# Convolution stage: three two-bank kernel buffers in PSUM instead of two, one pair sum moved from VectorE to GpSimd, and new places for the other stages' work

## The chip, the cores and the metric

One Trainium2 chip, one core of it. The time is device microseconds of one execution; the kernel before took 5519.98 us (median of three runs, 5519.80 to 5520.31). The input is eight images of 128 channels and 128 x 128 points in float32.

## The reference, cut to what matters

The first layer mixes tokens in 8 x 8 windows (attention and an MLP). The change does not touch it. The second layer, which the change is about, is

```python
enh  = conv3x3_depthwise(conv1x1(x))                       # 128 channels, 9 taps each
h    = conv3x3_grouped(x)          # 16 channels
h1, h2 = split(h, 2)
attn = conv1x1(h1 * h2) * attgamma + conv1x1(x)            # 16 coefficients per point
# kba: at every point the 16 coefficients give, by selfw, a 2 x 18 kernel for each
# pair of channels, applied to the 3 x 3 neighbourhood of enh; and, by selfb, a bias
x2   = kba(enh, attn) * ga1 + enh
out  = x2 + x
```

## The kernel before

**Tiling.** After the first layer (to about 1855 us) `convolve` (L773) works through 64 bands of 16 image rows, 8 to an image. A band is four chunks of 4 rows x 128 points, that is 512 columns, one PSUM bank. Channels lie on the 128 partitions.

**The main loop.** A chunk needs nine taps, so a band has 36 kernel products, numbered q = 0 to 35. For each, TensorE multiplies two 128 x 128 basis matrices by the band's 512 coefficients (`basis_kernels`, L1035) and leaves two banks of kernels: one for the channel itself, one for its partner in the pair. VectorE multiplies the two banks by the shifted rows of `enh` (`product`, L1259). A product goes either to a place in SBUF, tile `products`, or back over its own kernels in PSUM. In the second case VectorE adds it to the next product (`merge`, L1265; list `VECTOR_MERGES`, ten of them). Six more pairs are summed by GpSimd from SBUF (`merge`, L959; list `POOL_MERGES`). What is left, 20 terms of two halves each for a band, TensorE transposes and accumulates in a bank `ps_t` (`add_half`, L1055, four 128 x 128 transposes a half), together with one half for the input rows `x_own`. Then ScalarE copies the sum to SBUF (`sum_out`, L1149), TensorE adds the bias and transposes it back into the same bank (`back`, L1065 and L1067), and ScalarE copies the chunk out (`chunk_out`, L1154).

**The other stages.** Four bands are in work at once: l, m = l - 1, n = m - 1 and o = n - 1. TensorE computes the pointwise convolution (`pointwise`, L994), which ScalarE copies to `e0` (`e0_rows`, L1119); the grouped convolution (`group_taps`, L1017, 36 matmuls with 32 output rows each; the trace has two instructions for each float32 matmul, so 72 a band); and the coefficients (`coefficients`, L1024). ScalarE scales the nine depthwise taps of each half band (`tap_product`, L1174 and L1169), and GpSimd adds them up into `enh` (`add_tap`, L953), 16 additions a band; four tap buffers lie between the two. VectorE makes `h_prod` (L1279) and `att_lo` (L1283) once a band. SyncE's queue moves half of `h_sb` to other partitions, spreads the coefficients (16 small transfers), keeps two edge rows in DRAM, and loads and stores.

**Order.** Each engine's order is written out by hand. One pass over the 46 operations of VectorE's list `OPS` is a band; position in it is the slot. TensorE first issues in a slot the kernels whose buffer operation `slot` frees (`KERNEL_SLOT`), and waits for that operation. After that come the halves of `HALF_SLOT` and `X_SLOTS`, then `BACK_SLOTS`, `CONV_SLOTS`, the coefficients, and `PW_SLOTS`. A slot number of 46 or more means the next pass. ScalarE's taps stand at `TAP_PLACES` among the same slots; GpSimd's sums stand at `POOL_MERGE_PLACES` among its 16 additions.

**PSUM.** Eight banks: two kernel buffers of two banks (`ps_k`), two banks for sums (`ps_t`, chunk j uses number j % 2), one for the pointwise convolution (`ps_p`), one for the grouped convolution and the coefficients (`ps_m`). With two kernel buffers, the kernels of a product are issued after the operation that stands one before the last user of the other buffer.

Of the kernel before, what the change touches and what calls it, by code (L numbers as in the profile page):

```python
# [19 lines left out]
ALU = mybir.AluOpType  # L20
# [61 lines left out]

HALF_SLOT = {0: 10, 1: 7, 6: 6, 7: 6, 8: 11, 9: 9, 14: 11, 15: 11, 16: 12, 17: 12, 20: 15, 21: 19, 24: 15, 25: 18, 26: 25, 27: 25, 32: 22, 33: 22, 34: 22, 35: 22, 38: 26, 39: 28, 40: 31, 41: 31, 46: 33, 47: 32, 48: 37, 49: 37, 52: 35, 53: 35, 56: 38, 57: 38, 58: 44, 59: 44, 64: 44, 65: 43, 68: 47, 69: 48, 70: 47, 71: 47}


X_SLOTS = [16, 25, 38, 48]

# [685 lines left out]
def convolve(nc, prepared, x2, out):  # L773
# [4 lines left out]
    with ExitStack() as ctx:  # L778
# [33 lines left out]
        first_banks = [ps_p, ps_t[0], ps_t[1], ps_p, ps_t[0]]  # L812

# [43 lines left out]
        with nc.Block() as block:  # L857
            @block.sync
            def _(sp):
# [45 lines left out]
                def step(items, p):  # L905
                    l, m, n, o = items
                    b = 1 - p
                    if n is not None:
                        load_own(n, 0)
                    if o is not None:  # L910
                        store(o, CHUNKS - 1)
                    if l is not None and not (isinstance(l, int) and l == 0):
                        loads(l, p)
                    if n is not None:
                        load_own(n, 1)
                    if n is not None and not (isinstance(n, int) and n == bands - 1):
                        keep_edge(n, p)
                    if m is not None and not (isinstance(m, int) and m == 0):
                        fetch_edge(m, b)
                    if m is not None:  # L920
                        move_h2(m)
                    if n is not None:
                        store(n, 0)
                    if m is not None:
                        attention_rows(m, b)
                    if isinstance(m, int) and m == 0:
                        keep_top_rows()
                        fetch_edge(m, b)
                    if n is not None:
                        store(n, 1)  # L930
                        store(n, 2)
# [45 lines left out]
            def _(pe):  # L977
# [7 lines left out]
                def pointwise(m, p, c):  # L985
                    if c == 0:
                        pe.wait_ge(x_in[p], rounds(m, p, 16) + 16)
                    first = isinstance(m, int) and m == 0
                    if not first:
                        pe.wait_ge(e0_ready, PW_CHUNKS * m + c)  # L990
                    elif c > first_banks.index(first_banks[c]):
                        pe.wait_ge(e0_ready, first_banks.index(first_banks[c]) + 1)
                    lo, hi = PAD + CHUNK_ROWS * c, min(PAD + CHUNK_ROWS * (c + 1), XROWS)
                    nc.tensor.matmul((first_banks[c] if first else ps_p)[:, 0:W * (hi - lo)], pwT[:, :], xin[p][:, lo:hi, 1:W + 1],  # L994
                                     start=True, stop=True).then_inc(pw_done, 1)
# [10 lines left out]
                def group_taps(m, p, first, last):  # L1006

                    for i in range(first, last):
                        t, j = divmod(i, CHUNKS)
                        if i == 0:  # L1010
                            pe.wait_ge(x_in[p], rounds(m, p, 16) + 16)
                            pe.wait_ge(edges_ready, 1)
                            pe.wait_ge(grouped_ready, 1)
                            at_least(pe, att_lo_ready, m)
                        dy, dx = divmod(t, 3)
                        r = 1 + CHUNK_ROWS * j + dy
                        mm = nc.tensor.matmul(ps_m[32 * j:32 * j + 32, :], gT[:, t, :], xin[p][:, r:r + CHUNK_ROWS, dx:dx + W],  # L1017
                                              start=(t == 0), stop=(t == TAPS - 1))
                        if i == TAPS * CHUNKS - 1:
                            mm.then_inc(conv_done, 1)  # L1020
# [5 lines left out]
                def basis_kernels(n, p, q):  # L1026
                    if q == 0 and isinstance(n, int) and n == 0:
                        pe.wait_ge(basis_ready, 2)
                        pe.wait_ge(top_step, (TAPS - 3) * len(top_groups))
                    if q == 0:  # L1030
                        pe.wait_ge(att_in[p], rounds(n, p, 256) + 256)
                    j, t = divmod(q, TAPS)
                    at_least(pe, product_ready, SLOTS_IN_BAND * n + KERNEL_FREE[q])
                    for s in range(2):
                        mm = nc.tensor.matmul(ps_k[KERNEL_BUFFER[q] ^ (SWAPPED & p)][:, BANK * s:BANK * (s + 1)], basis[:, 2 * t + s, :],  # L1035
                                              att[p][:, j, :], start=True, stop=True)
                    mm.then_inc(k_done, 1)

                def add_half(n, j, half):
# [11 lines left out]
                    if start:  # L1051
                        at_least(pe, out_ready, CHUNKS * n + j - 1)
                    for r in range(CHUNK_ROWS):
                        rows = x_own[j // 2][:, CHUNK_ROWS * (j % 2) + r, :] if q == Q else products[:, PLACE[q], s, C * r:C * (r + 1)]
                        mm = nc.tensor.matmul(ps_t[j % 2][:, C * r:C * (r + 1)], rows, (ident, ident_swap)[s][:, :], is_transpose=True,  # L1055
                                              start=(start and r == 0), stop=(stop and r == CHUNK_ROWS - 1), skip_group_check=True)
# [51 lines left out]
            def _(act):  # L1108
# [3 lines left out]
                def e0_rows(m, p, c):  # L1112
# [4 lines left out]
                    lo, hi = PAD + CHUNK_ROWS * c, min(PAD + CHUNK_ROWS * (c + 1), XROWS)  # L1117
                    ps = (first_banks[c] if isinstance(m, int) and m == 0 else ps_p)[:, 0:W * (hi - lo)]
                    nc.scalar.activation(e0[p][:, lo:hi, 1:W + 1], ps.rearrange("c (h w) -> c h w", w=W), ACT.Identity,  # L1119
# [26 lines left out]
                def sum_out(n, j):  # L1146
                    act.wait_ge(sum_done, CHUNKS * n + j + 1)
                    at_least(act, back_done, CHUNKS * n + j - 1)
                    nc.scalar.activation(summedT[j % 2][:, :], ps_t[j % 2][:, :], ACT.Copy).then_inc(sumT_ready, 1)  # L1149

                def chunk_out(n, j):
                    act.wait_ge(back_done, CHUNKS * n + j + 1)
                    at_least(act, stored[j], 16 * n)
                    nc.scalar.activation(out_sb[:, CHUNK_ROWS * j:CHUNK_ROWS * (j + 1), :],  # L1154
                                         ps_t[j % 2][:, :].rearrange("c (h w) -> c h w", w=W), ACT.Copy).then_inc(out_ready, 1)

# [46 lines left out]
            def _(dve):  # L1203
# [38 lines left out]
                def product(n, p, q):  # L1242
# [9 lines left out]
                    dve.wait_ge(k_done, Q * n + q + 1)  # L1252
                    kernels = ps_k[KERNEL_BUFFER[q] ^ (SWAPPED & p)][:, :].rearrange("c (s h w) -> c s h w", s=2, w=W)
                    if q in VECTOR_MERGES:
# [7 lines left out]
                def merge(n, p, q):  # L1262
                    dve.wait_ge(product_ready, SLOTS_IN_BAND * n + OP_COUNT["product", q + 1])
                    both = products[:, PLACE[q + 1], :, :].rearrange("c s w -> c (s w)")
                    nc.vector.tensor_tensor(both, ps_k[KERNEL_BUFFER[q] ^ (SWAPPED & p)][:, :], both, ALU.add).then_inc(product_ready, 1)  # L1265

# [56 lines left out]
```

## Time and profile before

The profiled execution took 5518.02 us; its span, from the first to the last instruction, is 5515.9 us. The granted clock of TensorE was 0.996 of full speed over the span.

| engine | busy over the span | busy, 3000 to 4000 us |
|---|---|---|
| TensorE, matmuls | 5377.8 us (97%) | 982 of 1000 us |
| TensorE, weight loads | 3907.0 us (71%) | 663 |
| VectorE | 5149.3 us (93%) | 976 |
| ScalarE | 3324.5 us (60%) | 515 |
| GpSimd | 4237.7 us (77%) | 876 |

Matmuls overlap in the array and their ends are modelled, so a matmul's duration is longer than the time until the next one can start; where a sum is wanted, take the distance of starts. VectorE's operations overlap by some 0.1 us too. "Idle before" names what the engine waited for. The convolution stage is 64 alike bands, so a time for one band, multiplied by 64, is the stage.

### The profile page before, as it was taken

What the parts mean: (1) busy time and instruction counts of PE and PEld (TensorE: products, weight loads), DVE (VectorE), ACT (ScalarE), POOL (GpSimd) and SP (SyncE); (2) the same over time, 40 slices, a digit from 0 to 9 for tenths busy, and PEclk for the clock granted to TensorE, in tenths of its full rate; (3) what the DMA queues carried; (4) which work ended last, traced back from release to release, by engine and by line L of the source; (5) the groups of instructions that cost most, each with busy time, mean ns of one, the idle gap of its engine ahead of it and who ended that gap; (6) DMA issues with size and microseconds to landing.
All of it is one profiled execution on the core that took longest, in us unless ns stands there. A gap on an engine that the chain in (4) does not pass through costs nothing.

```text
span 5515.9 us, 112725 instructions
## 1 busy us (share of the span) xinstructions
PE 5377.8 (97%) x37904; PEld 3907.0 (71%) x37904; DVE 5149.3 (93%) x5424; ACT 3324.5 (60%) x4094; POOL 4237.7 (77%) x1958
## 2 busy tenths in 40 slices
PE   8999999999999799999999999999999999999998
PEld 7888888888888466666666666666666666666666
DVE  7888888888888699999999999999999999999999
ACT  6888888888888554555555554555555554555553
POOL 4655565556555688888888888888888888888886
PEclk9999999999999899999999999999999999999999
DMA  3222222222222222222222222222222222222221
GB/s 92 74 76 76 71 74 76 76 71 73 76 76 68 78 71 83 69 79 74 73 81 73 79 71 81 69 79 73 72 81 73 79 72 81 70 80 72 72 81 47
DMA packets 175616, 413.21 MB, mean 75 GB/s; under 512 B 37201, under 2 KB 58769, under 8 KB 175505
## 3 DMA queue, kind: packets, MB, share of 16 engines
q1 hardware_dynamic: 175568, 412.59, 24.5%
q8 instruction: 29, 0.48, 0.0%
q14 instruction: 19, 0.15, 0.0%
HBM read 228.94 MB, written 145.77 MB: 68 GB/s over the span
## 4 chain that ended last, share of the span: by engine, by line
PE 48%; DVE 12%; issue 5%; POOL 1%; DVEq 0%; ACT 0%; POOLq 0%
PE ps_k L1035 18%; PE ps_t L1055 15%; PE ps_m L1017 9%; DVE products L1259 6%; PE ps_p L994 3%; DVE products L1265 3%; DVE ps_k L1259 2%; PE ps_t L1067 2%; PE ps_t L1065 1%; POOL enh L953 1%; DVE h_prod L1279 1%; DVEq L133 0%; DVEq L1252 0%; DVEq L1277 0%; PE ps_t L994 0%
## 5 line engine op out<-in xcount | busy, mean ns | idle before, releaser
L953 POOL TENSOR_TENSOR enh<-enh,tap 128x1024 f32<-128x1024 f32 x1024 | 2263.0, 2210 | 68.0 <-ACT tap L1174 9.3
L1259 DVE TENSOR_TENSOR products<-ps_k,enh 128x1024 f32<-128x1024 f32 x1664 | 1997.7, 1218 | 53.3 <-PE ps_k L1035 39.6
L1035 PE MATMUL ps_k<-att,basis 128*128 128x512 f32 x4608 | 1682.8, 449 | 80.6 <-DVE products L1265 56.5
L1174 ACT ACTIVATE tap<-e,dw 128x1024 f32<-128x1024 f32 x1024 | 1147.5, 1146 | 313.2 <-POOL enh L953 312.0
L486 POOL TENSOR_TENSOR hidden_lo<-hidden,hidden_hi 128x1024 fp32r<-128x1024 f32 x256 | 693.3, 2729 | 717.5 <-DVE hidden_hi L691 717.5
L959 POOL TENSOR_TENSOR products<-products 128x1024 f32<-128x1024 f32 x384 | 915.9, 2392 | 418.2 <-DVE products L1259 418.2
L1035 PEld LDWEIGHTS ps_k<-att,basis 128*128 128x128 f32 x4608 | 707.1, 189 | 689.7 <-DVE products L1259 409.7
L1265 DVE TENSOR_TENSOR products<-ps_k,products 128x1024 f32<-128x1024 f32 x640 | 783.7, 1225 | 21.8
L1259 DVE TENSOR_TENSOR ps_k<-ps_k,enh 128x1024 f32<-128x1024 f32 x640 | 784.5, 1226 | 20.5 <-PE ps_k L1035 3.8
L1055 PE MATMUL ps_t<-ident_swap,products 128*128 128x128 f32 x5120 | 736.6, 272 | 0.7 <-POOL products L959 0.7
L1055 PE MATMUL ps_t<-ident,products 128*128 128x128 f32 x5120 | 724.9, 272 | 0.1
L1055 PEld LDWEIGHTS ps_t<-ident,products 128*128 128x128 f32 x5120 | 616.6, 141 | 113.0 <-DVE products L1265 0.3
L1055 PEld LDWEIGHTS ps_t<-ident_swap,products 128*128 128x128 f32 x5120 | 603.0, 141 | 68.9 <-issue 32.8
L1017 PE MATMUL ps_m<-xin,gT 128*32 128x512 f32 x4608 | 592.0, 606 | 0.0
L1149 ACT ACTIVATE summedT<-ps_t 128x512 f32<-128x512 f32 x256 | 153.2, 598 | 677.9 <-PE ps_t L1055 677.6
L1154 ACT ACTIVATE out_sb<-ps_t 128x512 f32<-128x512 f32 x256 | 152.4, 595 | 522.0 <-PE ps_t L1067 522.0
L656 ACT ACTIVATE hidden<-ring,bias 128x512 f32<-128x512 f32 x512 | 350.7, 690 | 176.0 <-PE ring L514 175.0
L708 DVE CAST x_hi<-xt 128x512 fp32r<-128x512 f32 x256 | 407.4, 1632 | 48.2 <-PE ring L514 48.1
L511 PE MATMUL ring<-x_hi,w_hi 128*128 128x512 f32 x1024 | 419.0, 409 | 6.3 <-ACT hidden L656 3.7
L491 POOL TENSOR_TENSOR x_lo<-xt,x_hi 128x512 fp32r<-128x512 f32 x256 | 377.9, 1497 | 55.6 <-DVE x_hi L708 55.6
L514 PE MATMUL ring<-x_lo,w_hi 128*128 128x512 f32 x1024 | 404.4, 395 | 0.4 <-POOL x_lo L491 0.4
L512 PE MATMUL ring<-x_hi,w_lo 128*128 128x512 f32 x1024 | 403.6, 394 | 0.0
(115 smaller groups left out, 7273.9 us busy)
## 6 DMA issues: line engine op xcount, KB each, us to landing
xin<-layer_out SPq DMA_DIRECT2D x64, 1280.0 KB, 7.3
xt<-in_x SPq DMA_DIRECT2D x128, 512.0 KB, 4.1
layer_out<-xo SPq DMA_DIRECT2D x128, 512.0 KB, 2.9
x_own<-layer_out SPq DMA_DIRECT2D x128, 512.0 KB, 4.0
out<-out_sb SPq DMA_DIRECT2D x256, 256.0 KB, 2.0
att<-att_hi SPq DMA_DIRECT2D x512, 32.0 KB, 2.0
att<-att_lo SPq DMA_DIRECT2D x512, 32.0 KB, 2.0
enh<-edge_rows SPq DMA_DIRECT2D x64, 130.0 KB, 2.1
```

The costliest lines, as they stand in the source:

```text
L486: nc.gpsimd.tensor_tensor(hidden_lo[:, h, :, :], hidden[:, h, :, :], hidden_hi[:, h, :, :].bitcast(FP32), ALU.subtract).then_inc(hidden_lo ...
L511: nc.tensor.matmul(out, w_hi[:, w, :], hi, start=start, stop=False)
L514: return nc.tensor.matmul(out, w_hi[:, w, :], lo, start=False, stop=stop)
L708: nc.vector.tensor_copy(windows(x_hi[:, PAIRS * h:PAIRS * (h + 1), :]), half_windows(xt[p], h)).then_inc(x_hi_ready, 1)
L953: nc.gpsimd.tensor_tensor(own, own, tap_sb[add % TAP_BUFFERS][:, 0:hi - lo, :], ALU.add).then_inc(dw_done, 1)
L959: nc.gpsimd.tensor_tensor(lead, lead, products[:, PLACE[q + 1], :, :], ALU.add).then_inc(pool_merged, 1)
L1017: mm = nc.tensor.matmul(ps_m[32 * j:32 * j + 32, :], gT[:, t, :], xin[p][:, r:r + CHUNK_ROWS, dx:dx + W], start=(t == 0), stop=(t == TAPS ...
L1035: mm = nc.tensor.matmul(ps_k[KERNEL_BUFFER[q] ^ (SWAPPED & p)][:, BANK * s:BANK * (s + 1)], basis[:, 2 * t + s, :], att[p][:, j, :], start ...
L1055: mm = nc.tensor.matmul(ps_t[j % 2][:, C * r:C * (r + 1)], rows, (ident, ident_swap)[s][:, :], is_transpose=True, start=(start and r == 0) ...
L1174: nc.scalar.activation(tap_sb[add % TAP_BUFFERS][:, 0:hi - lo, :], src, ACT.Copy, scale=dw[:, t:t + 1]).then_inc(tap_ready, 1)
L1259: nc.vector.tensor_tensor(out, kernels, enh[p][:, r:r + CHUNK_ROWS, dx:dx + W].unsqueeze(1).to_broadcast([C, 2, CHUNK_ROWS, W]), ALU.mult) ...
L1265: nc.vector.tensor_tensor(both, ps_k[KERNEL_BUFFER[q] ^ (SWAPPED & p)][:, :], both, ALU.add).then_inc(product_ready, 1)
```

## The change

The diff, with blank lines and renamed uses of the same expression left out:

```diff
-VECTOR_MERGES = (2, 6, 9, 11, 15, 18, 22, 27, 31, 33)
-POOL_MERGES = (0, 4, 13, 20, 24, 29)
+VECTOR_MERGES = (2, 6, 11, 16, 18, 22, 27, 31, 33)
+POOL_MERGES = (0, 4, 9, 13, 20, 24, 29)
+KERNEL_BUFFERS = 3
-KERNEL_BUFFER = {0: 0, 1: 1}
-for q in range(2, Q):
-    KERNEL_BUFFER[q] = KERNEL_BUFFER[FREEING[q - 2][1]]
-SWAPPED = KERNEL_BUFFER[FREEING[-2][1]]
-KERNEL_FREE = {q: FREEING[q - 2][0] if q >= 2 else FREEING[q - 2][0] - SLOTS_IN_BAND for q in range(Q)}
+KERNEL_BUFFER = {q: q for q in range(KERNEL_BUFFERS)}
+for q in range(KERNEL_BUFFERS, Q):
+    KERNEL_BUFFER[q] = KERNEL_BUFFER[FREEING[q - KERNEL_BUFFERS][1]]
+NEXT_ORDER = [KERNEL_BUFFER[q] for _, q in FREEING[-KERNEL_BUFFERS:]]
+KERNEL_FREE = {q: FREEING[q - KERNEL_BUFFERS][0] - (SLOTS_IN_BAND if q < KERNEL_BUFFERS else 0) for q in range(Q)}
...
-X_SLOTS = [16, 25, 38, 48]
+X_SLOTS = [13, 23, 38, 48]
-BACK_SLOTS = [21, 34, 40, 51]
+BACK_SLOTS = [14, 25, 41, 50]
-POOL_MERGE_PLACES = (0, 0.6000000000000001, 3.0, 6.0, 9.5, 10.9)
+POOL_MERGE_PLACES = (0, 1.5, 3, 5.5, 9.5, 11.5, 13.4)
-TAP_PLACES = ((0.5, 1.5, 3.0, 5.5, 10.5, 13.0, 13.5, 14.0, 19.5), (22.0, 24.5, 27.0, 28.0, 31.0, 35.5, 36.5, 36.5, 41.5))
-CLEAR_PLACE = 64
-H_PROD_SLOT = 27
-ATT_HIGH = 28
-ATT_LOW = 33
-CONV_SLOTS = [33, 33, 42, 42, 42, 42, 46, 46, 50, 50, 54, 54, 59, 59, 59, 59, 66, 66]
-COEFFICIENT_SLOT = 28
-PW_SLOTS = [17, 19, 27, 30, 36]
+TAP_PLACES = ((0.0, 0.0, 2.0, 3.0, 3.5, 6.0, 6.5, 7.0, 11.5), (15.0, 16.5, 19.0, 20.5, 24.5, 30.5, 31.0, 31.5, 37.4))
+CLEAR_PLACE = 58
+H_PROD_SLOT = 8
+ATT_HIGH = 6
+ATT_LOW = 12
+CONV_SLOTS = [24, 24, 26, 26, 26, 26, 33, 33, 33, 33, 36, 36, 41, 41, 41, 41, 45, 45]
+COEFFICIENT_SLOT = 8
+PW_SLOTS = [12, 13, 15, 17, 22]
...
-        ps_k = [bank(f"ps_k{i}", 2) for i in range(2)]
-        ps_t = [bank(f"ps_t{i}") for i in range(2)]
-        ps_p = bank("ps_p")
+        ps_k = [bank(f"ps_k{i}", 2) for i in range(KERNEL_BUFFERS)]
+        ps_t = bank("ps_t")
         ps_m = bank("ps_m")
...
 def step(items, p):                      # SyncE's queue, one pass
     load_own(n, 0)
-    store(o, CHUNKS - 1)
-    loads(l, p)
-    load_own(n, 1)
-    keep_edge(n, p)
-    fetch_edge(m, b)
-    move_h2(m)
-    store(n, 0)
-    attention_rows(m, b)
-    store(n, 1)
-    store(n, 2)
+    move_h2(m)
+    loads(l, p)
+    store(o, CHUNKS - 1)
+    load_own(n, 1)
+    attention_rows(m, b)
+    keep_edge(n, p)
+    fetch_edge(m, b)
+    store(n, 0)
+    store(n, 1)
+    store(n, 2)
...
 def pointwise(m, p, c):                  # now into ps_m
                     if not first:
                         pe.wait_ge(e0_ready, PW_CHUNKS * m + c)
+                        if c == 0:
+                            pe.wait_ge(att_lo_ready, m)
...
 def group_taps(m, p, first, last):       # i == 0
-                            at_least(pe, att_lo_ready, m)
+                                pe.wait_ge(e0_ready, PW_CHUNKS * m + PW_CHUNKS)
...
 def add_half(n, j, half):                # all chunks in the one bank ps_t
                     if start:
-                        at_least(pe, out_ready, CHUNKS * n + j - 1)
+                        at_least(pe, out_ready, CHUNKS * n + j)
```

`HALF_SLOT` is also new throughout. By it and the lists above, the sums of chunks 0 to 3 are transposed in slots 6 to 13, 16 to 23, 29 to 38 and 43 to 48, and go back in slots 14, 25, 41 and 50. Before, the sum of the next chunk could begin ahead of the way back of the one in hand (chunk 1 from slot 15, chunk 0 back in slot 21). VectorE's list now has 45 operations, 36 products and 9 sums; the transposed terms are still 20.

## Rows read from the trace of the kernel before

**Rows 1.** Page, busy time by engine (us, share, instructions).
```profile
PE 5377.8 (97%) x37904; PEld 3907.0 (71%) x37904; DVE 5149.3 (93%) x5424; ACT 3324.5 (60%) x4094; POOL 4237.7 (77%) x1958
```
**Rows 2.** Waits, 2000 to 5000 us (us in total, times, longest us).
```profile
POOL products L959 <- DVE products L1259: 330.1, 160, 4.2
PEld ps_k L1035 <- DVE products L1259: 327.2, 637, 0.9
...
DVE products L1259 <- PE ps_k L1035: 33.1, 106, 0.5
```
**Rows 3.** VectorE in order (start us, us), and `h_prod` 43 bands later.
```profile
3007.51 0.74 DVE L1279 SCALAR_TENSOR_TENSOR h_prod<-ps_m,bias_h,h_up 128x512 f32<-128x512 f32 x1
3008.17 1.22 DVE L1259 TENSOR_TENSOR ps_k<-ps_k,enh 128x1024 f32<-128x1024 f32 x1
3009.30 1.22 DVE L1259 TENSOR_TENSOR products<-ps_k,enh 128x1024 f32<-128x1024 f32 x1
3010.55 1.22 DVE L1265 TENSOR_TENSOR products<-ps_k,products 128x1024 f32<-128x1024 f32 x1
3011.69 3.55 DVE L1259 TENSOR_TENSOR products<-ps_k,enh 128x1024 f32<-128x1024 f32 x3
...
5432.11 0.74 DVE L1279 SCALAR_TENSOR_TENSOR h_prod<-ps_m,bias_h,h_up 128x512 f32<-128x512 f32 x1
```
**Rows 4.** VectorE, the first and the last product of the stage.
```profile
1900.56 2.36 DVE L1259 TENSOR_TENSOR products<-ps_k,enh 128x1024 f32<-128x1024 f32 x2 [8.63 <-DMA enh<-edge_rows]
...
5507.63 1.22 DVE L1259 TENSOR_TENSOR products<-ps_k,enh 128x1024 f32<-128x1024 f32 x1
```
**Rows 5.** TensorE in order of time, a stretch with each kind of work.
```profile
3024.57 0.40 PE L1065 MATMUL ps_t<-att,basis 128*128 128x512 f32 x1
...
3030.22 0.60 PE L1055 MATMUL ps_t<-ident,products 128*128 128x128 f32 x4
3030.58 1.21 PE L1035 MATMUL ps_k<-att,basis 128*128 128x512 f32 x4
3031.72 1.07 PE L1017 MATMUL ps_m<-xin,gT 128*32 128x512 f32 x8
3032.73 0.73 PE L1035 MATMUL ps_k<-att,basis 128*128 128x512 f32 x2
3033.30 1.03 PE L1055 MATMUL ps_t<-ident,products 128*128 128x128 f32 x8
3034.17 1.04 PE L1055 MATMUL ps_t<-ident_swap,products 128*128 128x128 f32 x8
```
**Rows 6.** TensorE in order of time, one chunk of the pointwise convolution.
```profile
3012.40 1.02 PE L994 MATMUL ps_p<-xin,pwT 128*128 128x512 f32 x2
3012.96 0.93 PE L1035 MATMUL ps_k<-att,basis 128*128 128x512 f32 x2
```
**Rows 7.** GpSimd in order of time, part of a band.
```profile
3024.09 13.64 POOL L953 TENSOR_TENSOR enh<-enh,tap 128x1024 f32<-128x1024 f32 x6
3037.70 4.74 POOL L959 TENSOR_TENSOR products<-products 128x1024 f32<-128x1024 f32 x2
3042.40 6.75 POOL L953 TENSOR_TENSOR enh<-enh,tap 128x1024 f32<-128x1024 f32 x3
```
**Rows 8.** ScalarE in order: a tap, and the two copies around one way back.
```profile
3021.30 1.15 ACT L1174 ACTIVATE tap<-e,dw 128x1024 f32<-128x1024 f32 x1
...
3023.15 0.60 ACT L1149 ACTIVATE summedT<-ps_t 128x512 f32<-128x512 f32 x1 [0.33 <-PE ps_t L1055]
3025.44 0.60 ACT L1154 ACTIVATE out_sb<-ps_t 128x512 f32<-128x512 f32 x1 [1.69 <-PE ps_t L1067]
```
**Rows 9.** SyncE's queue: the moves of `h_sb` in the same band.
```profile
3001.69 2.74 SPq L888 DMA_DIRECT2D h_up<-h_sb  x4
```
**Rows 10.** DMA issues by size (KB each, median us to landing).
```profile
xin<-layer_out SPq DMA_DIRECT2D x64, 1280.0 KB, 7.3
...
att<-att_hi SPq DMA_DIRECT2D x512, 32.0 KB, 2.0
```

More of the change, by code:

```diff
@@ L62 @@
 SLOTS_IN_BAND = len(OPS)
+KERNEL_BUFFERS = 3
 FREEING = [(OP_COUNT[op], op[1]) for op in OPS if op[0] == "merge" or op[1] not in VECTOR_MERGES]
-KERNEL_BUFFER = {0: 0, 1: 1}
-for q in range(2, Q):
-    KERNEL_BUFFER[q] = KERNEL_BUFFER[FREEING[q - 2][1]]
-SWAPPED = KERNEL_BUFFER[FREEING[-2][1]]
-KERNEL_FREE = {q: FREEING[q - 2][0] if q >= 2 else FREEING[q - 2][0] - SLOTS_IN_BAND for q in range(Q)}
+KERNEL_BUFFER = {q: q for q in range(KERNEL_BUFFERS)}
+for q in range(KERNEL_BUFFERS, Q):
+    KERNEL_BUFFER[q] = KERNEL_BUFFER[FREEING[q - KERNEL_BUFFERS][1]]
+NEXT_ORDER = [KERNEL_BUFFER[q] for _, q in FREEING[-KERNEL_BUFFERS:]]
+assert [NEXT_ORDER[i] for i in NEXT_ORDER] == list(range(KERNEL_BUFFERS))
+KERNEL_FREE = {q: FREEING[q - KERNEL_BUFFERS][0] - (SLOTS_IN_BAND if q < KERNEL_BUFFERS else 0) for q in range(Q)}
 KERNEL_SLOT = {q: KERNEL_FREE[q] - 1 for q in range(Q)}
@@ L92 @@
 POOL_TERM_COUNT = {q: i + 1 for i, q in enumerate(sorted(POOL_MERGES, key=LAST_HALF.get))}
-BACK_SLOTS = [21, 34, 40, 51]
+BACK_SLOTS = [14, 25, 41, 50]
 POOL_PLACES = 2 * (TAPS - 1)
-POOL_MERGE_PLACES = (0, 0.6000000000000001, 3.0, 6.0, 9.5, 10.9)
-TAP_PLACES = ((0.5, 1.5, 3.0, 5.5, 10.5, 13.0, 13.5, 14.0, 19.5), (22.0, 24.5, 27.0, 28.0, 31.0, 35.5, 36.5, 36.5, 41.5))
-CLEAR_PLACE = 64
-H_PROD_SLOT = 27
-ATT_HIGH = 28
-ATT_LOW = 33
-CONV_SLOTS = [33, 33, 42, 42, 42, 42, 46, 46, 50, 50, 54, 54, 59, 59, 59, 59, 66, 66]
-COEFFICIENT_SLOT = 28
-PW_SLOTS = [17, 19, 27, 30, 36]
+POOL_MERGE_PLACES = (0, 1.5, 3, 5.5, 9.5, 11.5, 13.4)
[7 more added lines that the diff above has]
+PW_SLOTS = [12, 13, 15, 17, 22]
+assert all(HALVES_OF[j][0][0] > BACK_SLOTS[j - 1] for j in range(1, CHUNKS)) and HALVES_OF[0][0][0] + SLOTS_IN_BAND > BACK_SLOTS[-1]
+assert all(BACK_SLOTS[j] > HALVES_OF[j][-1][0] for j in range(CHUNKS))
+assert PW_SLOTS[-1] < CONV_SLOTS[0] and SLOTS_IN_BAND <= CONV_SLOTS[-1] <= COEFFICIENT_SLOT + SLOTS_IN_BAND and COEFFICIENT_SLOT <= PW_SLOTS[0]
+assert BACK_SLOTS[-1] - SLOTS_IN_BAND < COEFFICIENT_SLOT
 def at_least(engine, semaphore, value):
@@ L909, in step @@
                         load_own(n, 0)
+                    if m is not None:
+                        move_h2(m)
+                    if l is not None and not (isinstance(l, int) and l == 0):
+                        loads(l, p)
                     if o is not None:
                         store(o, CHUNKS - 1)
[L912 to L913 removed]
                     if n is not None:
                         load_own(n, 1)
[L916 to L923 removed]
                     if m is not None:
@@ L928, in step @@
                         fetch_edge(m, b)
+                    if n is not None and not (isinstance(n, int) and n == bands - 1):
+                        keep_edge(n, p)
+                    if m is not None and not (isinstance(m, int) and m == 0):
+                        fetch_edge(m, b)
                     if n is not None:
+                        store(n, 0)
                         store(n, 1)
@@ L990, in pointwise @@
                         pe.wait_ge(e0_ready, PW_CHUNKS * m + c)
-                    elif c > first_banks.index(first_banks[c]):
-                        pe.wait_ge(e0_ready, first_banks.index(first_banks[c]) + 1)
+                        if c == 0:
+                            pe.wait_ge(att_lo_ready, m)
+                    elif c >= 3:
+                        pe.wait_ge(e0_ready, c - 2)
                     lo, hi = PAD + CHUNK_ROWS * c, min(PAD + CHUNK_ROWS * (c + 1), XROWS)
-                    nc.tensor.matmul((first_banks[c] if first else ps_p)[:, 0:W * (hi - lo)], pwT[:, :], xin[p][:, lo:hi, 1:W + 1],
+                    nc.tensor.matmul((first_banks[c] if first else ps_m)[:, 0:W * (hi - lo)], pwT[:, :], xin[p][:, lo:hi, 1:W + 1],
                                      start=True, stop=True).then_inc(pw_done, 1)
@@ L1029, in basis_kernels @@
                         pe.wait_ge(top_step, (TAPS - 3) * len(top_groups))
+                        pe.wait_ge(e0_ready, PW_CHUNKS)
                     if q == 0:
@@ L1034, in basis_kernels @@
                     for s in range(2):
-                        mm = nc.tensor.matmul(ps_k[KERNEL_BUFFER[q] ^ (SWAPPED & p)][:, BANK * s:BANK * (s + 1)], basis[:, 2 * t + s, :],
+                        mm = nc.tensor.matmul(ps_k[NEXT_ORDER[KERNEL_BUFFER[q]] if p else KERNEL_BUFFER[q]][:, BANK * s:BANK * (s + 1)], basis[:, 2 * t + s, :],
                                               att[p][:, j, :], start=True, stop=True)
@@ L1117, in e0_rows @@
                     lo, hi = PAD + CHUNK_ROWS * c, min(PAD + CHUNK_ROWS * (c + 1), XROWS)
-                    ps = (first_banks[c] if isinstance(m, int) and m == 0 else ps_p)[:, 0:W * (hi - lo)]
+                    ps = (first_banks[c] if isinstance(m, int) and m == 0 else ps_m)[:, 0:W * (hi - lo)]
                     nc.scalar.activation(e0[p][:, lo:hi, 1:W + 1], ps.rearrange("c (h w) -> c h w", w=W), ACT.Identity,
@@ L1252, in product @@
                     dve.wait_ge(k_done, Q * n + q + 1)
-                    kernels = ps_k[KERNEL_BUFFER[q] ^ (SWAPPED & p)][:, :].rearrange("c (s h w) -> c s h w", s=2, w=W)
+                    kernels = ps_k[NEXT_ORDER[KERNEL_BUFFER[q]] if p else KERNEL_BUFFER[q]][:, :].rearrange("c (s h w) -> c s h w", s=2, w=W)
                     if q in VECTOR_MERGES:
@@ L1264, in merge @@
                     both = products[:, PLACE[q + 1], :, :].rearrange("c s w -> c (s w)")
-                    nc.vector.tensor_tensor(both, ps_k[KERNEL_BUFFER[q] ^ (SWAPPED & p)][:, :], both, ALU.add).then_inc(product_ready, 1)
+                    nc.vector.tensor_tensor(both, ps_k[NEXT_ORDER[KERNEL_BUFFER[q]] if p else KERNEL_BUFFER[q]][:, :], both, ALU.add).then_inc(product_ready, 1)
                 def step(items, p):
```

15 lines of the change are left out of this document (8 added, 7 removed).

## The prediction, written before the changed kernel was run

> **What bounds the kernel now.** I read the page's busy times first, then the waits of the steady stretch, then each engine in order of time. The page puts TensorE at 97% and VectorE at 93% of the span [rows 1], which settles nothing: matmul durations overlap. The waits say more. In 3000 us, 53 bands, TensorE's weight loads for the kernels stood 637 times for a VectorE product, while VectorE stood for TensorE only 106 times, 33 us, 0.6 us a band [rows 2]. So each band mostly goes at VectorE's pace, and TensorE is the one that comes early. VectorE's stage is also nearly all of what the change touches: its first product starts at 1900.56 and its last at 5507.63 [rows 4], and 43 bands take 5432.11 - 3007.51 = 2424.6 us [rows 3], so a band takes 56.39 us.
>
> What does VectorE need for a band, if nothing holds it? By distance of starts [rows 3]: product into PSUM 1.13 (3008.17 to 3009.30), product ahead of its sum 1.25, the sum 1.14, so a summed pair costs 3.52; a product with no sum 1.13; `h_prod` 0.66, and `att_lo`, which is the same kind, as much. Before: 10 x 3.52 + 16 x 1.13 + 1.3 = 54.6 us. The other 1.8 us of the 56.39 are lost: 0.6 in the waits named above, the rest in delays too short for the wait list, most of them, I take it, kernels that come a little late, because with two buffers TensorE may only be one operation behind.
>
> TensorE's need for a band [rows 5, 6]: 36 kernel pairs at 0.57 (two in 3030.58 to 3031.72) = 20.5; 44 half transpositions (40 of terms, 4 of input rows) at 0.435 (two in 3033.30 to 3034.17) = 19.1; the grouped convolution, nine runs of eight at 1.01 = 9.1; five pointwise chunks and the coefficients at 0.56 = 3.4; four ways back at one matmul (0.285) and four transpositions (0.435) = 2.9. Sum 55.0. A half just ahead of kernels takes only 0.36 (3030.22 to 3030.58), and 17 or so a band stand there: -1.3. That gives 53.7, and it may be 1 us too much, because the distances of kernels and of the grouped convolution can hold small waits. So TensorE is within 1 to 2.5 us of VectorE, and nothing that VectorE saves beyond that can reach the clock.
>
> GpSimd [rows 7]: an addition 2.27 (six in 13.61), a sum 2.35. Before: 16 x 2.27 + 6 x 2.35 = 50.4, and it waits for VectorE 330 us in 53 bands, 6.2 a band [rows 2]; together 56.6, which is the band.
>
> **The rule and the row.** The Trainium skill says in "Perfetto Trace Analysis", section "Identifying the Most-Contended Engine", that matmul occupancy is a poor measure and that TensorE's headroom should be judged by weight-load busy time. The row has 71% [rows 1], so by the rule TensorE would need some 40 us a band and could never bind; my sum from distances of starts says 53.7. By the rule the result would be VectorE's bound below with certainty; I don't follow it, and leave the sum as it is.
>
> **The change, part by part.**
>
> *One sum less on VectorE.* The pair of q = 9 goes to GpSimd; those of 15 to 17 only change partners. 9 x 3.52 + 18 x 1.13 + 1.3 = 53.3 us, which is 1.26 less a band. That is the floor of the stage.
>
> *The third kernel buffer.* Every product now has its kernels issued at least two operations ahead (2.27 us less 0.57 for the pair) instead of one. A heavy slot of TensorE (slots 3, 17, 29, 31, 35 hold 1.9 to 2.6 us of work against 1.13 of VectorE) no longer shows on VectorE by itself. At best all 1.8 us of losses go, at worst none. TensorE's extra lead gives nothing when its own sum is the longer one. VectorE at 53.3 and TensorE at 52.7 to 53.7, each with waits of its own, should end close above the larger: I take 54.0 a band, that is 0.7 of the 1.8 stay, since both engines will now be about equally full.
>
> *One sum more on GpSimd.* 16 x 2.27 + 7 x 2.35 = 52.8, in a band of 54.0. It fits with 1.2 to spare. Its first addition of a pass waits for two taps on ScalarE, which start when VectorE begins the band (1.23 + 1.15, some 2.5 us [rows 8] for the second), and the last ends near 55: it overlaps the next pass by 1, so that it hardly rests. Its sums come late by it: q = 13 is ready at about 25.2 us and TensorE wants it in slot 19 at 24.5; q = 20 at 36.5 against 36.1. Such waits of 0.4 to 0.7 lie where TensorE has a light slot. Cost taken: 0; up to 1 us if TensorE has no slack. Durations of VectorE's operations I leave alone: sums read one operand from PSUM as before.
>
> *One sum bank.* A handover is: copy 0.60, way back 0.87 (3024.57 to the copy's start at 3025.44), copy 0.60 = 2.1 us at least, 2.9 as it stood at 3023.15 to 3026.04 [rows 5, 8]; with a tap of 1.15 in front of each copy 4.4. The new lists leave from the last half of a chunk to the first of the next three slots (13 to 16, 48 to 51, that is 3.4 us), six (23 to 29) and five (38 to 43). Two are long enough with a tap in front of both copies, the other two only with 1.3 us of ScalarE's delay. Inside them TensorE has kernels and pointwise work, so a delay costs only what exceeds that. Taken: 0.2 a band, inside the 54.0; bounds 0 and 2.3 (one tap in front of a copy in each short handover).
>
> *The attention chain moves from slots 20 to 33 to slots 0 to 12.* The grouped convolution ends in slot 0, ScalarE copies, SyncE issues four moves. Before, `h_prod` started 5.8 us after the first move's issue [rows 3, 9] without a wait; the moves need 2.74 to issue [rows 9] and about 2.0 to land [rows 10]. After, the convolution ends about 3.3 us into the band, the copy at 4.2, the moves have landed at 9.0; VectorE reaches slot 8's end at 10.3. It is covered by 1.3 us. Were it late, VectorE itself, with all its products queued behind, would stand. Taken 0, up to 1.0. The coefficients then wait for `h_prod` (0.7 after slot 8), and behind them TensorE has halves and kernels that are wanted two operations later: 0.
>
> *Pointwise in ps_m.* Its first chunk waits for `att_lo`, 0.66 after slot 12; TensorE spends 0.57 of it on kernels. Chunks 0 and 1 stand one slot apart, with a ScalarE copy between them; three halves (1.3 us) cover it. 0.2, bound 1.2 (one tap ahead of that copy).
>
> *SyncE's queue.* `move_h2` is now second, so it can't stand behind an edge or a store. The band's load of 1280 KB, behind it, is issued at 7.0 and needs 7.3 [rows 10]: 14.3, against 16.2 for slot 12 with `att_lo`. 0, bound 0.5. Edge rows and stores have half a band to spare. In the first band the load is issued after the first `h_sb` copy; VectorE's start hangs on the edge rows [rows 4], so I change nothing there, with a bound of 5 us in all.
>
> **The sum.** 56.39 - 54.0 = 2.39 us a band, 64 bands: 153 us. 5518.02 - 153 = 5365 us; the median shown is 2 us above the profiled execution: 5367.
>
> **The rivals.**
> 1. *TensorE becomes the bound.* For: its 53.7, and that it keeps all its work. It adds the waits for `att_lo`, `e0` and the two short handovers, 1.0 to 2.5 together: 54.7 to 56.2, middle 55.4, that is 5457. Against: many of its waits fall where it was early anyway.
> 2. *GpSimd becomes the bound.* 52.8 and the 2.5 of the first tap, if that is not overlapped: 55.3, 5450. Against: it may run over into the next pass.
> 3. *The third buffer brings nothing*: the losses are not late kernels. 55.1, 5440.
> 4. *The one sum bank makes it slower.* From TensorE's 53.7 the kernel is slower once the four handovers leave it idle for over 0.7 each; at 1.0 each, 57.7 a band, it is 5604. For: ScalarE is in order, and a tap that waits for GpSimd stands in front of a copy for longer than its own 1.15. Against: the taps placed before each copy are due well behind the additions that free their buffers.
>
> **How the numbers follow.** Mine 0.62 (53.3 to 54.7 a band, 5322 to 5412); TensorE 0.18; GpSimd 0.06; no use of the buffer 0.05; the slower case 0.09. The range goes from the floor 53.3 (5322) to 55.4 (5457), where the first rival's middle lies. What a measurement of this kernel tells from no change is about 0.2%, 11 us: within it only the edge of rivals 1 and 4, 0.03; slower 0.07; faster 0.90.
>
> **What would show it.** In the trace after, `h_prod` to `h_prod` should be 54.0. VectorE waiting for TensorE should fall under 0.3 us a band, and GpSimd's wait from 6.2 to under 2. The weight loads of kernels should stand less for VectorE than before. I am wrong if VectorE stands for `ps_k` by over 1 us a band (rival 1), for `moved` at `h_prod`, if GpSimd's sums hold up the transpositions, or if TensorE idles before the first half of a chunk with ScalarE's `out_sb` as releaser (rival 4).

## The result, and the profile after

The changed kernel takes 5359.64 us (median of 4 runs, 5359.02 to 5362.06) against 5520.15 us before: ratio 0.971, 95% interval 0.9693 to 0.9727. The forecast was 5367 us, faster, range 5322 to 5457. The profiled execution is the slowest of the four, 5362.06 us; its span is 5360.3 us, 155.6 less than before.

The page, busy time by engine, against [rows 1]: VectorE has 64 instructions less, GpSimd 64 more, TensorE as many.

```profile
PE 5267.2 (98%) x37904; PEld 3936.0 (73%) x37904; DVE 5032.0 (94%) x5360; ACT 3322.0 (62%) x4094; POOL 4373.8 (82%) x2022
```

VectorE in order of time, `h_prod` in one band and 41 bands later, against [rows 3]:

```profile
3051.43 0.74 DVE L1301 SCALAR_TENSOR_TENSOR h_prod<-ps_m,bias_h,h_up 128x512 f32<-128x512 f32 x1
...
5257.04 0.74 DVE L1301 SCALAR_TENSOR_TENSOR h_prod<-ps_m,bias_h,h_up 128x512 f32<-128x512 f32 x1
```

2205.6 us over 41 is 53.80 us a band, 2.59 less than before; forecast was 54.0. The busy times of 2000 to 5000 us of the changed kernel (us from the start, width, then TensorE, its weight loads, VectorE, ScalarE, GpSimd, granted clock, DMA share, GB/s):

```profile
2000.00:5000.00 3000.00, 2985.52 (x19634) 2105.78 (x19627) 2967.68 (x2622) 1612.56 (x1895) 2867.33 (x1283) 1.00 0.26 79
```

TensorE is free for 14.5 us in 56 bands, 0.26 a band, and that is one wait: the first half of chunk 0 for ScalarE's copy of the chunk before. The waits of the same stretch, against [rows 2]:

```profile
POOL enh L971 <- ACT tap L1196: 97.6, 56, 1.9
PEld ps_k L1057 <- DVE products L1281: 88.9, 105, 0.9
...
PE ps_t L1077 <- ACT out_sb L1176: 14.5, 56, 0.3
DVE ps_k L1281 <- PE ps_k L1057: 12.5, 56, 0.3
```

The weight loads of kernels stood for VectorE 327 us for its products alone before and stand 89 now. In this stretch GpSimd no longer waits for VectorE at all, only once a band for the first tap, 1.74 us; under 2 was forecast. VectorE stands for kernels for 0.23 us a band; under 0.3 was forecast.

The stage did not start where it had. VectorE's first product, against [rows 4]:

```profile
1910.14 2.35 DVE L1281 TENSOR_TENSOR products<-ps_k,enh 128x1024 f32<-128x1024 f32 x2 [15.68 <-PE ps_k L1057]
```

From the first product to the end of the last VectorE needed 3608.3 us before and needs 3442.9 now: 165.4 less. The start is 9.6 us later (1910.14 against 1900.56), what follows the last product 0.2 longer. 165.4 - 9.6 - 0.2 = 155.6, all of the difference.

### The profile page after: what moved, and what is told of

Same layout as the page of the kernel before. It is cut to its first block, busy times and chain, and to the rows that moved or that the text cites. A ratio compares the mean times of both kernels' runs of the same rounds, so it can differ in the third digit from the quotient of the medians.

```text
span 5360.3 us, 113060 instructions
## 1 busy us (share of the span) xinstructions
PE 5267.2 (98%) x37904; PEld 3936.0 (73%) x37904; DVE 5032.0 (94%) x5360; ACT 3322.0 (62%) x4094; POOL 4373.8 (82%) x2022
## 4 chain that ended last, share of the span: by engine, by line
PE 60%; ACT 2%; DVE 2%; issue 1%; POOL 0%; ACTq 0%; DVEq 0%; POOLq 0%
PE ps_t L1077 23%; PE ps_k L1057 19%; PE ps_m L1038 10%; PE ps_m L1014 5%; PE ps_t L1089 2%; ACT tap L1196 1%; PE ps_m L1045 1%; PE ps_t L1087 1%; DVE products L1281 1%; ACT out_sb L1176 1%; POOL enh L971 0%; DVE ps_k L1281 0%; DVE basis L360 0%; DVE products L347 0%; DVE products L1287 0%
## 5 line engine op out<-in xcount | busy, mean ns | idle before, releaser
L1281 DVE TENSOR_TENSOR products<-ps_k,enh 128x1024 f32<-128x1024 f32 x1728 | 2049.5, 1214 | 21.1 <-PE ps_k L1057 16.4
L1057 PE MATMUL ps_k<-att,basis 128*128 128x512 f32 x4608 | 1640.4, 450 | 15.9 <-DVE products L1281 11.1
L1057 PEld LDWEIGHTS ps_k<-att,basis 128*128 128x128 f32 x4608 | 744.7, 190 | 502.2 <-issue 156.3
L977 POOL TENSOR_TENSOR products<-products 128x1024 f32<-128x1024 f32 x448 | 1073.6, 2396 | 29.3 <-DVE products L1281 29.3
L1287 DVE TENSOR_TENSOR products<-ps_k,products 128x1024 f32<-128x1024 f32 x576 | 704.6, 1223 | 17.7
L1281 DVE TENSOR_TENSOR ps_k<-ps_k,enh 128x1024 f32<-128x1024 f32 x576 | 704.7, 1223 | 15.0 <-PE ps_k L1057 14.8
L1077 PE MATMUL ps_t<-ident_swap,products 128*128 128x128 f32 x5120 | 715.0, 272 | 0.0
L1077 PEld LDWEIGHTS ps_t<-ident,products 128*128 128x128 f32 x5120 | 605.7, 141 | 124.8 <-ACT out_sb L1176 41.7
L1038 PE MATMUL ps_m<-xin,gT 128*32 128x512 f32 x4608 | 578.6, 605 | 1.3 <-ACT e L1141 1.3
L1014 PE MATMUL ps_m<-xin,pwT 128*128 128x512 f32 x630 | 300.4, 558 | 6.1 <-ACT e L1141 4.0
```

The costliest lines, as they stand in the source:

```text
L977: nc.gpsimd.tensor_tensor(lead, lead, products[:, PLACE[q + 1], :, :], ALU.add).then_inc(pool_merged, 1)
L1014: nc.tensor.matmul((first_banks[c] if first else ps_m)[:, 0:W * (hi - lo)], pwT[:, :], xin[p][:, lo:hi, 1:W + 1], start=True, stop=True).t ...
L1057: mm = nc.tensor.matmul(ps_k[NEXT_ORDER[KERNEL_BUFFER[q]] if p else KERNEL_BUFFER[q]][:, BANK * s:BANK * (s + 1)], basis[:, 2 * t + s, :], ...
L1077: mm = nc.tensor.matmul(ps_t[:, C * r:C * (r + 1)], rows, (ident, ident_swap)[s][:, :], is_transpose=True, start=(start and r == 0), stop= ...
L1281: nc.vector.tensor_tensor(out, kernels, enh[p][:, r:r + CHUNK_ROWS, dx:dx + W].unsqueeze(1).to_broadcast([C, 2, CHUNK_ROWS, W]), ALU.mult) ...
L1287: nc.vector.tensor_tensor(both, ps_k[NEXT_ORDER[KERNEL_BUFFER[q]] if p else KERNEL_BUFFER[q]][:, :], both, ALU.add).then_inc(product_ready, 1)
```

## The experiments

The first set stood beside the changed kernel itself:

> The changed kernel once more, beside the three variants of this set, so that a few us can be told apart: 5360 us, whatever the theory. Its trace should again have a band of 53.8 us (VectorE, h_prod to h_prod) and VectorE's first product near 1910 us.

Measured: 5359.31 us (5358.9 to 5361.43), band 53.80, first product 1906.6. So the start varies by 3 to 4 us between executions; the band does not.

**Which engine sets the pace now.** Two experiments lighten one engine each; a third lightens both. They leave out part of the sum.

```diff
                 def merge(n, p, q):       # VectorE
+                    width = {33: BANK}.get(q, 2 * BANK)
-                    both = products[:, PLACE[q + 1], :, :].rearrange("c s w -> c (s w)")
+                    both = products[:, PLACE[q + 1], :, :].rearrange("c s w -> c (s w)")[:, 0:width]
...
```

> The changed kernel, with VectorE's sum of q = 33 over one bank instead of two (half of that sum is left out): VectorE needs 0.53 us a band less, 52.8 instead of 53.3; nothing else changes. Theory A, TensorE has become the pace-maker (its matmuls are busy 99.5% in the trace after): 0 to -8 us against the changed kernel. Theory B, VectorE still sets the pace and the 0.5 us over its floor are short hand-overs: the whole 0.53 x 64 = -34 us. Theory C, GpSimd sets it (its need is 52.2 us and it waits 1.9 for taps): 0.

Measured: 5359.43 us, 0.1 from the changed kernel beside it; band 53.80. Theory B is out; A and C forecast this alike. A good part of VectorE's gain shows as waits: its standing for kernels, for products in place, rose from 12.5 to 32.0 us in 56 bands, 0.35 of the 0.53 a band.

```diff
+LEFT_OUT = ((17, 1), (26, 1))
...
 def add_half(n, j, half):
-                    for r in range(CHUNK_ROWS):
+                    for r in range(0 if (q, s) in LEFT_OUT else CHUNK_ROWS):
```

> The changed kernel without the transposition of the second half of q = 17 and of q = 26 (these two halves are left out of the sum): TensorE needs 0.87 us a band less. Theory A, TensorE sets the pace: down to VectorE's floor of 53.3 us a band, 0.5 less, -25 to -32 us against the changed kernel. Theory B, VectorE does: 0 to -6 us. Theory C, GpSimd: 0.

Measured: 5339.5 us, 19.8 less; band 53.46. That is theory A's engine, but short of its 25 us: TensorE sets the pace for 0.34 us only, and then VectorE's need of some 53.3 takes over. Waits of this kernel, 2000 to 5000 us:

```profile
PE ps_k L1058 <- DVE products L1288: 12.7, 56, 0.3
DVE ps_k L1282 <- PE ps_k L1058: 1.3, 8, 0.2
```

VectorE, which stood for kernels for 12.5 us before this edit, hardly stands any more, and TensorE now stands for a sum of VectorE, 0.23 us a band. The other 0.30 of the 0.87 shows in no wait of TensorE's matmuls; where it went is open.

```diff
+width = {33: BANK, 27: BANK}.get(q, 2 * BANK)     # VectorE's sums
+LEFT_OUT = ((17, 1), (26, 1))                     # TensorE's halves
```

> The changed kernel with both of its fuller engines lightened: VectorE's sums of q = 27 and 33 over one bank instead of two, and the second halves of q = 17 and 26 not transposed. Needs: VectorE 52.2 us a band, TensorE some 52.7, GpSimd 52.2 and the wait for the first tap. Theory A, GpSimd stands right behind them: the band stops at 52.7 to 53.2, 5290 to 5322 us. Theory B, GpSimd has room: 52.3 to 52.6, under 5285.

Measured: 5307.47 us, band 52.97. With VectorE out of the way 0.83 of TensorE's 0.87 us arrives: 53.80 less 0.87 is 52.93. So TensorE's need alone gives this band, and theory A's range holds without its reason having been shown. Whether GpSimd stands close behind is open: it is busy for 2916.22 of 3000 us, it waits 0.47 us a band for the first tap (the row below, of 2000 to 5000 us) and 0.37 for a product, and it was not lightened by itself.

```profile
POOL enh L972 <- ACT tap L1197: 26.9, 56, 0.6
```

**Which part of the change brought it.**

```diff
-KERNEL_BUFFERS = 3
+KERNEL_BUFFERS = 2
+        spare = bank("spare", 2)          # takes ps_k[2]'s part in first_banks
```

> The changed kernel with two kernel buffers again (the two banks stay empty after the first band), every other place, the nine sums and the one sum bank kept. Theory A, the third buffer takes up TensorE's uneven slots: the band goes from 53.8 to 55.1 at least (5440 us), more where the heavy slots of the new places fall, up to 57 (5565). Theory B, the gain is the sum moved off VectorE, the buffer is idle: within 10 us of 5360.

Measured: 5781.14 us, ratio to before 1.047 (1.0454 to 1.0486), band 60.51, worse than either theory. Waits of this kernel, 2000 to 5000 us, in 50 bands:

```profile
PEld ps_k L1058 <- DVE products L1282: 378.8, 645, 1.2
DVE products L1282 <- PE ps_k L1058: 245.8, 406, 1.2
```

Both engines wait for each other in turn: VectorE stands eight times a band for kernels, the kernels' weight loads thirteen times for VectorE's products. I read it as VectorE late behind TensorE's full slots and TensorE late behind VectorE in the light ones; the rows don't sort the waits by slot. The new places were made for three buffers: with them the third is worth 422 us, which can't be added to a worth of the places. Three buffers with the old places were not run.

```diff
-VECTOR_MERGES = (2, 6, 11, 16, 18, 22, 27, 31, 33)
-POOL_MERGES = (0, 4, 9, 13, 20, 24, 29)
-POOL_MERGE_PLACES = (0, 1.5, 3, 5.5, 9.5, 11.5, 13.4)
+VECTOR_MERGES = (2, 6, 9, 11, 16, 18, 22, 27, 31, 33)
+POOL_MERGES = (0, 4, 13, 20, 24, 29)
+POOL_MERGE_PLACES = (0, 1.5, 5.5, 9.5, 11.5, 13.4)
+# every slot from 13 on is one higher; the halves of q = 9 are those of q = 10
```

> The changed kernel with the sum of q = 9 on VectorE again (ten and six, thirteen places, the lists shifted by one slot behind it), three buffers kept. VectorE needs 54.6 us a band again, GpSimd 2.35 less. Theory A, the buffer gives back most of the losses by itself: 54.7 to 55.0 a band, 5417 to 5437 us. Theory B, TensorE's need of 53.5 and its waits hold it apart from VectorE: over 55.5, 5470. Theory C, the sum's place does not matter because TensorE sets the pace: 53.8, 5360.

Measured: 5412.63 us, ratio 0.9804 (0.9789 to 0.9819), band 54.60, theory A and 4 us under its range. `h_prod` in this kernel, 42 bands apart (2293.13 / 42 = 54.60):

```profile
3011.31 0.74 DVE L1301 SCALAR_TENSOR_TENSOR h_prod<-ps_m,bias_h,h_up 128x512 f32<-128x512 f32 x1
...
5304.44 0.74 DVE L1301 SCALAR_TENSOR_TENSOR h_prod<-ps_m,bias_h,h_up 128x512 f32<-128x512 f32 x1
```

That is VectorE's need with ten sums, 54.6, and VectorE stands for kernels for only 1.2 us in 3000: three buffers with places made for them take away all 1.8 us of losses. It splits the gain of a band: 56.39 to 54.60, 1.79, by buffer and places; 54.60 to 53.80, 0.80, by the sum that moved, of whose 1.26 us TensorE lets 0.80 through.

**What held the kernel before.** Here the prediction had VectorE.

```diff
                 def merge(n, p, q):       # kernel before
+                    width = {9: 16}.get(q, 2 * BANK)
...
```

> The kernel before, two kernel buffers and its own places, with VectorE's sum of q = 9 over 16 columns instead of 1024 (that sum is left out but for these): VectorE needs 1.05 us a band less, 53.5 instead of 54.6. Theory A, in the kernel before VectorE sets the pace and the 1.8 us above its need stay: the band falls by the same 1.05 to 55.3, 5453 us. Theory B, two buffers and TensorE's uneven slots hold the band already, and the lost sum mostly turns into waits for kernels: a band of 55.9 or more, 5490 us or more.

Measured: 5519.63 us, ratio 0.9998 (0.9989 to 1.0008). Theory B, and to its end: nothing at all came of the 1.05. VectorE in this kernel around the shortened sum:

```profile
3046.49 0.17 DVE L1266 TENSOR_TENSOR products<-ps_k,products 128x16 f32<-128x16 f32 x1
3047.27 1.23 DVE L1259 TENSOR_TENSOR ps_k<-ps_k,enh 128x1024 f32<-128x1024 f32 x1 [0.61 <-PE ps_k L1035]
3048.71 1.23 DVE L1259 TENSOR_TENSOR products<-ps_k,enh 128x1024 f32<-128x1024 f32 x1 [0.20 <-PE ps_k L1035]
```

The sum takes 0.17 us, and the next two products stand for their kernels, 0.81 together. From the product ahead of the sum, at 3045.24, to the second product behind it are 3.47 us; with a full sum 1.25, 1.14 and 1.13 make 3.52. So nearly all of the saving was gone two operations on. Over 2000 to 5000 us VectorE's standing for kernels rose from 34.8 to 76.3 us, 0.78 a band, and the weight loads' standing for VectorE stayed at 327 and 211: at this place TensorE set the pace.

```diff
+LEFT_OUT = ((17, 0), (26, 0))             # kernel before, halves not transposed
...
```

> The kernel before without the transposition of the first half of q = 17 and of q = 26 (two halves are left out of the sum): TensorE needs 0.87 us a band less; they stand in slots 22 and 35. Theory A, VectorE sets the pace where they stand: 0 to -10 us against 5520. Theory B, TensorE does: -40 to -56 us. With two buffers the first of them stands in a slot of 2.3 us of TensorE's work, the second in one of 1.4, so by B most comes from the first.

Measured: 5521.37 us, ratio 1.0000 (0.999 to 1.0009), theory A. Waits of this kernel, 2000 to 5000 us:

```profile
PEld ps_k L1036 <- DVE products L1260: 349.6, 690, 0.9
PEld ps_k L1036 <- DVE products L1266: 231.6, 319, 1.0
```

And the one of the kernel before that [rows 2] leaves out:

```profile
PEld ps_k L1035 <- DVE products L1265: 210.6, 265, 0.9
```

Against 327.2 and 210.6 the weight loads stand 43.4 us longer for VectorE, 0.82 a band: nearly all of the 0.87. VectorE's own standing for products into SBUF stayed at 33. So in the kernel before neither less work on VectorE at q = 9 nor less on TensorE in slots 22 and 35 was worth anything: in the one place TensorE set the pace, in the others VectorE.

```diff
+                    width = {q: BANK for q in VECTOR_MERGES}.get(q, 2 * BANK)   # kernel before
...
```

> The kernel before, all ten of VectorE's sums over one bank instead of two (half of each sum is left out): VectorE needs 5.3 us a band less, 49.3 instead of 54.6. Lightening one of them brought nothing. Theory A, that was only its place (behind q = 9 TensorE was late already), and VectorE does set the pace elsewhere in the band: the band falls to TensorE's need, 53.7 or a little over, 5350 to 5375 us. Theory B, with two buffers TensorE's order holds nearly the whole band: it falls by less than 1 us, 5460 us or more.

Measured: 5454.41 us, ratio 0.9878 (0.9863 to 0.9893), band 55.37: of 5.3 us taken from VectorE, 1.0 arrives. Theory B but for 6 us. Two waits of this kernel, 2000 to 5000 us:

```profile
PEld ps_k L1035 <- DVE products L1259: 350.0, 590, 0.9
...
DVE products L1259 <- PE ps_k L1035: 176.0, 540, 0.7
```

By these rows VectorE now stands ten times a band for kernels, and the kernels' weight loads still stand eleven times for VectorE.

**The start of the stage.** TensorE in the changed kernel, before the first product:

```profile
1885.38 2.08 PE L1014 MATMUL ps_m<-xin,pwT 128*128 128x512 f32 x2 [2.08 <-DMA xin<-layer_out]
1888.73 2.08 PE L1014 MATMUL ps_m<-xin,pwT 128*128 128x512 f32 x2 [1.28 <-ACT e L1141]
...
1899.82 9.53 PE L1038 MATMUL ps_m<-xin,gT 128*32 128x512 f32 x64 [1.31 <-ACT e L1141]
```

Band 1's five pointwise chunks go one by one through `ps_m`, each behind a copy, and 64 instructions of its grouped convolution follow, where there were 24 before; only then, at 1909.28, come band 0's kernels. The load of band 1 has moved behind the moves of `h_sb`, which is the 2.08.

```diff
+                    if isinstance(l, int) and l == 1:
+                        loads(l, p)                      # SyncE: ahead of move_h2
...
-                    first = isinstance(m, int) and m == 0   # pointwise, e0_rows: banks of first_banks
+                    first = isinstance(m, int) and m <= 1
...
                     if first:
+                        for c in range(3):
+                            pointwise(l, p, c)
                         coefficients(m)
...
+                            if isinstance(m, int) and m == 1:
+                                pe.wait_ge(att_lo_ready, 1)   # group_taps, instead of e0_ready
```

> The start of the stage was 9.6 us later in the changed kernel (first product 1910.14 against 1900.56), waiting for kernels. Theory A: what delays it is band 1's pointwise and grouped convolution, which now stand ahead of band 0's kernels in TensorE's order and share one bank with a chunk's copy between them (five chunks, 1885.4 to 1899.8, then 9.5 us of grouped convolution). Here band 1 is loaded first, its pointwise chunks use three banks, three of them ahead of the coefficients. By A the grouped convolution starts at about 1888 and the first product falls to 1902, where the edge rows arrive: 5352 us, 8 less than the changed kernel. Theory B (rival): the start is held by ScalarE's and GpSimd's chain for band 1, which this does not touch, or what the first band gains is lost in the second: 5360.

Measured: 5355.66 us (5354.78 to 5358.42) against 5359.31 beside it: 3.6 less, where A had 8. The first product is at 1900.00 and waits for the edge rows again, so it was TensorE's work ahead of the kernels that held it, as A says. The 64 instructions of grouped convolution still stand there, so they alone did not hold it; what differs besides are the chunks one by one, the late load and the clock (last section). The edits were made together, and which of them brought how much is open. But the first band then takes 59.0 us instead of 55.8 in the changed kernel beside it. GpSimd in this kernel shows why:

```profile
1883.43 27.82 POOL L973 TENSOR_TENSOR enh<-enh,tap 128x1024 f32<-128x1024 f32 x12
1911.21 2.35 POOL L979 TENSOR_TENSOR products<-products 128x1024 f32<-128x1024 f32 x1
```

It is busy with band 0's additions, the sum of q = 0 ends at 1913.56, and TensorE stood 4.7 us for it. So of 6.6 us of earlier start (1906.6 to 1900.0) half arrives, and rival B holds for the other half.

**Two tries at TensorE's order.** They rest on distances of starts: blocks of grouped convolution and halves that do not precede kernels look dear.

```diff
-CONV_SLOTS = [24, 24, 26, 26, 26, 26, 33, 33, 33, 33, 36, 36, 41, 41, 41, 41, 45, 45]
+CONV_SLOTS = [26, 26, 26, 26, 27, 27, 33, 33, 33, 33, 40, 40, 40, 40, 40, 40, 45, 45]
```

> The changed kernel with the grouped convolution's 72 instructions in four blocks (24, 16, 24, 8) instead of six (8, 16, 16, 8, 16, 8), the same work. By distance of starts a block costs TensorE some 0.1 us on entry (kernels to grouped 0.645 against 0.55) and 0.1 on leaving. Theory A, these are real and TensorE sets the pace: two blocks less save 0.2 to 0.38 us a band, 5336 to 5347 us. Theory B, the distances are only how the profile models starts: 5360. Theory C, blocks of 24 (2.8 us) outlast the third buffer and VectorE stands behind them: over 5365.

Measured: 5395.86 us, ratio 0.9775 (0.9762 to 0.9789), band 54.38: theory C, 36.5 us slower. VectorE stands for kernels 0.95 us a band, where it stood 0.23. TensorE is free for 51.4 us of 3000 (busy 2948.63), 0.9 a band; without that it would be at 53.45, hardly under the 53.5 of the changed kernel. As far as busy time tells, the price of a block is mostly not real.

```diff
-    38: 29, 39: 31, 40: 29, 41: 35            # HALF_SLOT, with e4_fill's edits
+    38: 28, 39: 30, 40: 29, 41: 34
+    lead = isinstance(items[2], int) and items[2] == 0   # GpSimd, one pass: sum of q = 0 first
```

> The changed kernel with three edits, all of its work kept: the start of the stage as in e4_fill; in the first pass GpSimd's sum of q = 0 ahead of its first addition (there TensorE stood 4.7 us for it); and three halves (19 first, 19 second, 20 second) moved one slot ahead, each to between two pairs of kernels. By distance of starts, a half directly ahead of kernels takes 0.355 instead of 0.435 us. Theory A, this is real: 0.1 to 0.24 us a band, 6 to 15 us, and 2 from GpSimd: 5339 to 5348 us. Theory B, only how starts are modelled: 5354, band 53.8.

Measured: 5356.92 us (5355.16 to 5361.46), band 53.80 as before the edit: theory B. TensorE's wait for GpSimd in the first band fell from 4.7 to 2.1 us, but the band takes 58.8 us, so GpSimd's sum moved ahead brought nothing worth naming either. This kernel and e4_fill, the fastest two with all of the work, lie within each other's spread.

## Why the prediction was right, and where it was not

**VectorE's floor (53.3).** Shown: with three buffers and ten sums the band is 54.60 for a need of 54.6; with nine, and TensorE lightened, 53.46 for 53.3.

**"Each band mostly goes at VectorE's pace."** Wrong. The kernel before had no one engine whose work set it: 1.05 us off VectorE in one place, or 0.87 off TensorE in two, gave 0, and 5.3 off VectorE gave 1.0. The count of waits (637 against 106 [rows 2]) misled me; it counts who came late, and with two buffers each is late in turn. Rival 3 counted the saving of 1.26 a band by itself (5440 us); in that kernel it need not have shown at all.

**The third buffer (at best 1.8, taken 1.1).** Undersized. It is 1.79, measured by the kernel with ten sums, buffer and places together. The reason given was that a lead of two operations takes up the uneven slots; the two-buffer variant agrees with it from the other side. The list of heavy slots left out 26, 33 and 41, with 16 instructions of grouped convolution each (2.0 us by [rows 5]); no term hangs on it.

**TensorE's need (52.7 to 53.7) and the 54.0.** The need was right in size: 53.80 less 0.26 idle is 53.5, and TensorE is the pace-maker now. Its terms are less exact than their sum: [rows 6] put a pointwise chunk at 0.56, but the kernels behind that one take 0.77 us (to 3013.73) where others take 0.55, so a full chunk costs near 0.8, and other terms are as much too high. Rival 1 was right in its engine, with 53.80 instead of 55.4, because it added 1.0 to 2.5 us of waits and 0.26 came. The sign that I gave for it, VectorE standing for `ps_k` by over 1 us a band, did not appear (0.23), so it would have missed a TensorE that sets the pace by half a microsecond. I had kept 0.7 of losses over VectorE's floor; it is 0.5, and it is TensorE's excess, not losses. That the 54.0 came so close for another reason than the one given is in part luck.

**Rule against row.** By the Trainium skill, "Perfetto Trace Analysis", section "Identifying the Most-Contended Engine", TensorE's headroom is judged by the busy share of its weight loads (and by the share of peak arithmetic, which I did not work out); 73% against VectorE's 94% would clear TensorE. They were 70% busy in the steady stretch (2105.78 of 3000), and yet of the two engines lightened there TensorE was the one that moved the time. For this mix of short transpositions and weight loads for each, the measurement decides against the weight-load share. The busy share of matmuls, 99.5%, is no safe guide either, and there the section is right: it was 98.3% before, where less work on TensorE brought nothing. TensorE has as many instructions in both kernels, and yet they are busy for 55.4 us of a band before (2947.67 of 3000) and 53.5 now, so that time contains waits.

**GpSimd, the sum bank, the attention chain, `ps_m`.** Costed at 0 to 0.2 each. GpSimd: right, its one wait is for the tap. The sum bank: 0.26 a band, taken 0.2. The rest shows no wait on TensorE's matmuls or VectorE in the steady stretch.

**The start (taken 0, bound 5).** Mis-sized: 9.6 us in one execution, 6.1 in another. I had looked at the load's place in SyncE's queue, 2.1 us of it, and not at the pointwise chunks and the grouped convolution of band 1 that moved in front of band 0's kernels. The bands took 64 x 0.2 = 13 us less than forecast and the start some 6 to 10 more, and the two partly cancelled: 5367 is nearer than its terms, by luck.

## What to carry to other kernels

Where two engines hand buffers back and forth with one operation's lead, neither engine's sum need be the bound, and work taken from one at a single place may bring nothing. Here the third buffer, with places made for it, made the fuller engine's sum the time, to 0.1 us in 54.6. To find the pace-maker lighten each engine by under a microsecond on the chip: counts of waits and weight-load shares both named the wrong one here. When places are moved in a software pipeline, read the first passes by themselves: what is hidden in the steady state stands in the open there.

## What the runs showed of the hardware

In the start of the stage the granted clock was half, that is 1.2 GHz of its two levels, for at least 15 us (1885 to 1900), after TensorE had stood 3.44 us for `h_prod` and 2.08 for the load; in 1870 to 1880 us it had been 1.00. A row of the changed kernel (columns as above):

```profile
1890.00:1900.00 10.00, 6.36 (x11) 1.72 (x14) 4.29 (x6) 6.99 (x9) 5.77 (x3) 0.50 0.43 133
```

A pointwise chunk took 2.08 us there against 1.02 at full clock [rows 6], so the five chunks one behind another were dearer than any row of the steady state said. The kernel before was slowed there too: 0.60 in 1885 to 1890 us and 0.69 in 1890 to 1900. Whether the clock fell because of the waits, and what it would have been without them, was not tried by itself. In e4_fill, where three of the chunks come in a row, the granted clock was 0.50 in 1885 to 1890 us, behind a wait of 5.44, and 0.99 in 1890 to 1900; the 64 instructions of grouped convolution took 7.68 us there, against 9.53 in the changed kernel.
